# A recommendation tower on one core: gathers on GpSimd spaced by small products, the first pairs' layer 0 moved between slots, and another layout of the pair tiles

## The chip, the cores and the metric

The kernel runs on one core of a Trainium2 chip. The metric is the device time of one execution in microseconds. Five engines matter: TensorE (PE, and PEld for its weight loads), VectorE (DVE), ScalarE (ACT), GpSimd (POOL) and SyncE (SP), which here only issues DMAs.

## The reference, cut to what matters

```python
e = stack([tbl_f[ids[:, f]] for f in range(32)], axis=1)      # [1024, 32, 16], gathered from 32 tables
x0 = xk = e
for W in (W0, W1, W2):                                        # W0 [32, 32, 64], W1 and W2 [32, 64, 64]
    xk = relu(einsum('bmd,bhd,mhk->bkd', x0, xk, W))          # layers 0, 1, 2
    outs.append(sum(xk, axis=2))
h = concatenate([outs..., dense_ctx], axis=1)                 # [1024, 208]
y = relu(relu(h @ W_top1 + b_top1) @ W_top2 + b_top2) @ W_top3
```

Each layer multiplies every field m of x0 with every field h of the state, element by element, and contracts the products with a weight for each (m, h). All of it is float32.

## The kernel before

**Pairs.** The columns (1024 rows of the batch times 16 = 16384) are cut into 16 pairs of 1024 columns, numbered 0 to 15. For each pair p the steps are these.

- *Gathers* (POOL, L325): 16 indirect DMAs, 128 table rows each, into `gath[p % 2]`. In all 256 gathers; those of pair p are numbers 16p to 16p + 15.
- *Store* (SP, L235): when all 16 have landed, `gath` is written twice to scratch in HBM (`x_scratch`, 64 rows of 1024 columns: the 32 fields twice, so that a rotated read needs no wrap). SP then waits for the landing.
- *Loads for layer 0* (SP): `x0c` (L280; for pairs 1 and 2 directly from `gath`, L245), then `x_rep` and two tiles of `x_rot` (L287, L291), 512 KB each. `x_in` counts the landing of these three.
- *Pair tiles* (SP, L298): `m_rep`, four DMAs of 1 MB that lay the 32 fields over 128 partitions, 8 KB for each partition. Three pairs fit in `m_rep`.
- *Layer 0*: a product `x_rot * x_rep` into `prod_pool` (`layer0_product`, for pair 1 on DVE at L417, for all later pairs on POOL at L336); two `pair_sums` on PE (L576, from `x0c`), each squared by ACT (L473); then PE's `layer0_sums` and `layer0_rest` (L596, L640), and ACT's `relu0` (L452).
- *Layers 1 and 2*: for each, ACT (L480) replicates the state into PSUM (`rep`), DVE (L399) multiplies a tile of `m_rep` with `rep`, 128x2048 at a time, and PE (L660) contracts the product in four matmuls. That is a *unit*; 8 units make one layer of one pair. From slot 3 on, one of the 8 is multiplied by POOL (L336, `prod_pool<-m_rep,xb`) from a copy of `rep` in SBUF (`xb`), in slots 29 to 31 two.

**Slots.** One layer of one pair is a slot, and every engine goes through them in the same written order: (layer 1, pair 0), (2, 0), (1, 1), (1, 2), (2, 1), (1, 3), (2, 2), ... So for p from 2 on, slot 2p - 1 is layer 1 of pair p, and slot 2p is layer 2 of pair p - 1. In slot 2p - 1 layer 0 of pair p + 1 is made as well: PE has `pair_sums(p + 1, 0)` after unit 0, `pair_sums(p + 1, 1)` after unit 3, and the rest at the slot's end. Slots 0 to 2 are arranged by hand: layer 0 of pair 1 stands in slot 0 before and behind its last unit (`layer0_sums(1)`, `layer0_rest(1)`), and that of pair 2 at the end of slot 1 and in slot 2.

**Order.** There is no scheduler. Each engine's block is a program of its own, executed in order; semaphores tie them together. POOL's queue holds three things in one order: gathers, its own units, and layer 0 products. A gather that waits, or a product that waits for `x_in`, holds back all that stands behind it. POOL's program in and before the slots is:

```python
gather(0, 16);  wait l0_done >= 1;  gather(16, 16)
for n in range(7):  wait unit_ready >= 2 * n + 1;  gather(32 + 4 * n, 4)
layer0_product(2)
for n in range(7, 10):  wait unit_ready >= 2 * n + 1;  gather(32 + 4 * n, 4)
ahead = 72
for i in range(3, NS):
    odd slot (layer 1, pair p):  units(i); gather(ahead, 4); layer0_product(p + 1); gather(ahead + 4, 2)
    even slot (layer 2):         gather(ahead, 5); units(i); gather(ahead + 5, 5)
```

So 72 gathers are issued before slot 3 is reached, and then 16 for each two slots.

## Time and profile before

| | us |
|---|---|
| median of 3 runs | 660.87 (660.35 to 661.81) |
| the profiled execution's own time | 659.91 |
| its span, first to last instruction | 658.1 |
| PE busy | 602.4 (92%) |
| DVE busy | 528.1 (80%) |
| POOL busy | 453.6 (69%) |
| ACT busy | 391.4 (59%) |

The profile is of one execution. Its times count from the start of its span; 1.81 us of the execution's own time lie outside it. A row of the timeline gives start, duration, engine and line, what is written and read, how many instructions are merged in it, and in brackets the idle time before it with what ended it. "issue" means that nothing the profile shows was waited for, and "remote" that the semaphore's update matches no instruction's recorded end. In the table of stretches each engine has its busy time and count, then follow TensorE's granted clock (1.00 is 2.4 GHz, 0.50 is 1.2 GHz), the share of time for which the DMA engines were busy, and GB/s.

### The profile page before, as it was taken

The numbers are of one execution on the slowest core, as the hardware profiler recorded it, in microseconds if no ns is written. First come the engines' busy times: TensorE is split into PE (matmuls) and PEld (weight loads), VectorE is DVE, ScalarE is ACT, GpSimd is POOL, SyncE is SP. The second block draws the span as 40 slices with busy tenths as digits, with TensorE's granted clock in tenths as the row PEclk, the third lists the DMA queues.
The fourth block names the chain that finished last, engine by engine and source line by source line (L and its number), as shares of the span: only waits on it lengthen the run. The fifth ranks groups of instructions, "written<-read, shape, count | busy, mean of one in ns | idle before, by whom it ended". The sixth has DMA issues, their size and how long they took to land.

```text
span 658.1 us, 7277 instructions
## 1 busy us (share of the span) xinstructions
PE 602.4 (92%) x2634; PEld 192.6 (29%) x2634; DVE 528.1 (80%) x281; ACT 391.4 (59%) x631; POOL 453.6 (69%) x306
## 2 busy tenths in 40 slices
PE   1765497789999999999999999999999999999998
PEld 1211122223333333333333333333333333333343
DVE  1065198499989898999999898989898999899700
ACT  0200254386767676767677776858586867677231
POOL 5367365488989788878788878888598855267300
PEclk9997698989999999999999999999999999999999
DMA  4193969594959595968778695949494939450000
GB/s 134 40 226 71 238 168 248 155 236 112 249 129 238 118 249 127 233 148 211 162 204 177 186 198 162 219 146 218 136 222 113 246 92 248 109 97 0 9 8 1
DMA packets 38413, 103.44 MB, mean 157 GB/s; under 512 B 13764, under 2 KB 22856, under 8 KB 30184
## 3 DMA queue, kind: packets, MB, share of 16 engines
q1 hardware_dynamic: 28900, 98.72, 60.8%
q0 software_dynamic: 8192, 2.11, 3.4%
q10 hardware_dynamic: 1284, 2.13, 1.0%
q8 instruction: 21, 0.34, 0.2%
q14 instruction: 16, 0.13, 0.1%
HBM read 97.69 MB, written 4.20 MB: 155 GB/s over the span
## 4 chain that ended last, share of the span: by engine, by line
PE 84%; another core or an unknown queue 5%; issue 4%; ACT 2%; POOL 2%; ACTq 1%; DVE 1%; DMA 1%; SPq 0%; DVEq 0%; POOLq 0%
PE acc L660 65%; PE pair_sum L596 8%; PE pair_sum L576 5%; POOL gath L325 2%; PE pair_sum L640 2%; PE rep L746 2%; PE rep L738 1%; PE rep L739 1%; ACT rep L480 1%; DVE prod L399 1%; ACTq L445 1%; DMA gath<-in_tables,rows_sb 0%; ACT prod_pool L501 0%; SPq L245 0%
## 5 line engine op out<-in xcount | busy, mean ns | idle before, releaser
L399 DVE TENSOR_TENSOR prod<-m_rep,rep 128x2048 f32<-128x2048 f32 x223 | 494.5, 2281 | 56.3 <-DMA m_rep<-x_scratch 28.5
L660 PE MATMUL acc<-prod,w_sb 128*64 128x512 f32 x1792 | 406.0, 602 | 18.3 <-DVE prod L399 13.7
L480 ACT COPY rep<-state 32x512 f32<-32x512 f32 x488 | 283.4, 581 | 59.3 <-DVE prod L399 43.3
L325 POOL DMA_INDIRECT gath<-in_tables,rows_sb x256 | 243.1, 949 | 101.5 <-issue 75.2
L660 PEld LDWEIGHTS acc<-prod,w_sb 128*64 128x64 f32 x1792 | 124.9, 138 | 290.9 <-issue 274.4
L336 POOL TENSOR_TENSOR prod_pool<-m_rep,xb 128x2048 f32<-128x2048 f32 x32 | 146.3, 4571 | 51.7 <-PE acc L660 26.1
L336 POOL TENSOR_TENSOR prod_pool<-x_rot,x_rep 128x2048 f32<-128x2048 f32 x14 | 64.1, 4578 | 9.4 <-DMA x_rot<-x_scratch 9.2
L660 PE MATMUL acc<-prod_pool,w_sb 128*64 128x512 f32 x256 | 60.4, 592 | 0.0
L473 ACT ACTIVATE sums_sq<-pair_sum 128x1024 f32<-128x1024 f32 x30 | 30.8, 1027 | 45.5 <-PE pair_sum L576 25.4
L452 ACT ACTIVATE state<-pair_sum 128x512 f32<-128x512 f32 x16 | 9.6, 597 | 74.2 <-PE pair_sum L640 58.9
L576 PE MATMUL pair_sum<-x0c,sel_sb 32*128 32x512 f32 x120 | 35.7, 672 | 13.8 <-issue 9.5
L409 DVE TENSOR_REDUCE z_sb<-state 128x32 f32<-128x512 f32 x48 | 32.6, 681 | 19.3 <-ACT state L452 17.5
L596 PE MATMUL pair_sum<-sums_sq,w_sb 128*64 128x512 f32 x128 | 30.3, 594 | 0.0
L490 ACT COPY xb<-rep 128x1024 f32<-128x1024 f32 x29 | 29.4, 1013 | 0.9
L660 PEld LDWEIGHTS acc<-prod_pool,w_sb 128*64 128x64 f32 x256 | 18.4, 137 | 36.5 <-issue 36.5
L596 PE MATMUL pair_sum<-prod_pool,w_sb 128*64 128x512 f32 x120 | 28.3, 592 | 0.0
L452 ACT ACTIVATE state<-acc 128x512 f32<-128x512 f32 x32 | 19.1, 602 | 14.2 <-PE acc L660 14.1
L468 ACT ACTIVATE xsq<-x0c 64x512 f32<-64x512 f32 x15 | 9.5, 631 | 25.0 <-DMA x0c<-gath 24.6
L576 PEld LDWEIGHTS pair_sum<-x0c,sel_sb 32*128 32x128 f32 x120 | 9.4, 191 | 40.2 <-issue 35.0
L640 PE MATMUL pair_sum<-xsq,wdiag_sb 32*64 32x512 f32 x60 | 16.1, 613 | 0.0
L417 DVE TENSOR_TENSOR prod_pool<-x_rot,x_rep 128x2048 f32<-128x2048 f32 x1 | 2.3, 2336 | 15.5 <-issue 15.5
L596 PEld LDWEIGHTS pair_sum<-sums_sq,w_sb 128*64 128x64 f32 x128 | 9.0, 137 | 18.3 <-issue 18.0
(52 smaller groups left out, 102.9 us busy)
## 6 DMA issues: line engine op xcount, KB each, us to landing
m_rep<-x_scratch SPq DMA_DIRECT2D x64, 1024.0 KB
x_rot<-x_scratch SPq DMA_DIRECT2D x30, 512.0 KB
x_rep<-x_scratch SPq DMA_DIRECT2D x15, 512.0 KB
gath<-in_tables,rows_sb POOLq DMA_INDIRECT x256
x_scratch<-gath SPq DMA_DIRECT2D x31, 128.0 KB
x0c<-x_scratch SPq DMA_DIRECT2D x26, 64.0 KB
w_sb<-in_w ACTq DMA_DIRECT2D x2, 512.0 KB
m_rep<-z_sb SPq DMA_DIRECT2D x12, 64.0 KB, 2.3
```

The source lines that it names most:

```text
L325: pool.indirect_dma_start(out=gath[p % 2][:, g, :], out_offset=None, in_=tables, in_offset=bass.IndirectOffsetOnAxis(ap=rows_sb[:, n:n + 1 ...
L336: nc.gpsimd.tensor_tensor(prod_pool[:, at % POOL_RING], in0, in1[:, None, :].to_broadcast([128, 2, PAIR]), ALU.mult).then_inc(pool_ready, 1)
L399: nc.vector.tensor_tensor(prod[:, number % RING], in0, in1[:, None, :].to_broadcast([128, 2, PAIR]), ALU.mult).then_inc(unit_ready, 1)
L409: nc.vector.tensor_reduce(out=z_sb[l][:, p, :], in_=state[l][:, :].rearrange("k (b d) -> k b d", d=D), op=ALU.add, axis=AX_X).then_inc(z_r ...
L452: nc.scalar.activation(state[l][:, :], acc_of[l][:, :], RELU).then_inc(state_ready[l], 1)
L473: nc.scalar.activation(sums_sq[:, n, :], pair_sum[:, :], SQUARE).then_inc(sq_ready, 1)
L480: last = nc.scalar.copy(rep[v][M * q:M * q + M, CHUNK * a:CHUNK * a + CHUNK], state[l - 1][K * a + M * v:K * a + M * v + M, :])
L490: nc.scalar.copy(xb[i % 2][:, :], rep[0][:, :]).then_inc(xb_ready, 1)
L576: last = nc.tensor.matmul(pair_sum[:, CHUNK * a:CHUNK * a + CHUNK], sel_sb[M * a:M * a + M, n, :], x0c[p % 2][M * a:M * a + M, :], start=T ...
L596: last = nc.tensor.matmul(acc0[K * a:K * a + K, :], w, src[:, CHUNK * a:CHUNK * a + CHUNK], start=start, stop=stop)
L640: last = nc.tensor.matmul(acc0[K * a:K * a + K, :], wdiag_sb[M * a:M * a + M, :], xsq[M * a:M * a + M, :], start=False, stop=True)
L660: last = nc.tensor.matmul(acc[K * a:K * a + K, :], w, src[:, k, CHUNK * a:CHUNK * a + CHUNK], start=start and k == 0, stop=stop and k == 1)
```

## The change

Six edits:

1. POOL's gathers ahead of slot 3. Gathers 16 to 19 are issued as soon as the first squares are there (`first_sq`), before `l0_done`. The other gathers up to number 63 no longer wait for `unit_ready`: they go in blocks of four (`BURST`), and behind each block of four POOL makes a product of 128x256 elements of weights into a tile `unread` that nobody reads; each such product waits for the one before it. `ahead` starts at 4 * 16 = 64 where it was 72.
2. The layer 0 product of pair 2 goes from POOL to DVE, in slot 2 behind its unit 3. That of pair 1, which is DVE's already, goes from the start of slot 1 to behind slot 1's unit 1.
3. PE's layer 0 of pair 1 goes out of slot 0 into slot 1 (`pair_sums` behind `copy_state(1, 0)` and unit 0, sums behind unit 2, rest behind unit 3); that of pair 2 lies wholly within slot 2.
4. ACT's order follows: `relu_slot(0)` ahead of the squares of pair 1, `replicate(1, 1)` between them.
5. In slot 3 alone PE makes the `pair_sums` of pair 3 behind units 2 and 4, not 0 and 3.
6. `m_rep`: partition n holds the fields n // 4 + t, not 2 * (n // 8) + t. The DMA reads 32 starts with 4 copies of each, 4 KB apart, 8 KB each (they overlap), where it read 16 starts with 8 copies. The bytes are the same, and the weights are laid out to match.

```diff
-                    src = bass.AP(row.tensor, row.offset, [[2 * PAIR, 128 // T], [0, T], [1, 2 * PAIR]])
+                    src = bass.AP(row.tensor, row.offset, [[PAIR, M], [0, Q], [1, 2 * PAIR]])
...
             gather(0, FIRST_RUN)
+            pool.wait_ge(first_sq, 1)
+            gather(FIRST_RUN, BURST)
 
             pool.wait_ge(l0_done, 1)
-            gather(FIRST_RUN, 2 * GPP - FIRST_RUN)
-
-            for n in range(7):
-                pool.wait_ge(unit_ready, 2 * n + 1)
-                gather(2 * GPP + 4 * n, 4)
-            layer0_product(2)
-            for n in range(7, 10):
-                pool.wait_ge(unit_ready, 2 * n + 1)
-                gather(2 * GPP + 4 * n, 4)
-            ahead = 72
+            pool.wait_ge(w1_in, 16)
+            ahead = 4 * GPP
+            for k, n in enumerate(range(FIRST_RUN + BURST, ahead, BURST)):
+                gather(n, BURST)
+
+                after(pool, burst_out, k)
+                nc.gpsimd.tensor_tensor(unread[:, :, :], w_sb[1][:, 0, 0:T // 2, :], w_sb[1][:, 1, 0:T // 2, :],
+                                        ALU.mult).then_inc(burst_out, 1)
...
+                    if (i, n) in ((1, 1), (2, 3)):
+                        layer0_product(i)
...
             relu0(0)
+            relu_slot(0)
             square_x(1)
             square(1, 0)
+            replicate(1, 1)
             square(1, 1)
-            relu_slot(0)
-            replicate(1, 1)
```

On POOL, from slot 3 to the start of slot 7 (`gath0` takes the gathers of even pairs, `gath1` those of odd ones). Before:

```order
L325 DMA gath0<-in_tables,rows_sb 128x16 x3
L336 TENSOR_TENSOR prod_pool<-m_rep,xb1 128x2048 [waits l0_done,m_in2_3,xb_ready]
L325 DMA gath0<-in_tables,rows_sb 128x16 x4
L336 TENSOR_TENSOR prod_pool<-x_rot,x_rep 128x2048 [waits pool_used,x_in]
L325 DMA gath0<-in_tables,rows_sb 128x16 x4
L325 DMA gath1<-in_tables,rows_sb 128x16 [waits x0_stored]
L325 DMA gath1<-in_tables,rows_sb 128x16 x2
L336 TENSOR_TENSOR prod_pool<-m_rep,xb0 128x2048 [waits pool_used,m_in1_3,xb_ready]
L325 DMA gath1<-in_tables,rows_sb 128x16 x5
L336 TENSOR_TENSOR prod_pool<-m_rep,xb1 128x2048 [waits pool_used,m_in0_3,xb_ready]
L325 DMA gath1<-in_tables,rows_sb 128x16 x4
L336 TENSOR_TENSOR prod_pool<-x_rot,x_rep 128x2048 [waits pool_used,x_in]
```

And the same stretch now:

```order
L340 TENSOR_TENSOR prod_pool<-m_rep,xb1 128x2048 [waits l0_done,m_in2_3,xb_ready]
L329 DMA gath0<-in_tables,rows_sb 128x16 [waits x0c_in0,x0_stored]
L329 DMA gath0<-in_tables,rows_sb 128x16 x3
L340 TENSOR_TENSOR prod_pool<-x_rot,x_rep 128x2048 [waits l0_done,x_in]
L329 DMA gath0<-in_tables,rows_sb 128x16 x7
L340 TENSOR_TENSOR prod_pool<-m_rep,xb0 128x2048 [waits pool_used,m_in1_3,xb_ready]
L329 DMA gath0<-in_tables,rows_sb 128x16 x5
L340 TENSOR_TENSOR prod_pool<-m_rep,xb1 128x2048 [waits pool_used,m_in0_3,xb_ready]
L329 DMA gath1<-in_tables,rows_sb 128x16 [waits x0_stored]
L329 DMA gath1<-in_tables,rows_sb 128x16 x3
L340 TENSOR_TENSOR prod_pool<-x_rot,x_rep 128x2048 [waits pool_used,x_in]
```

The first product with `x_rot` is that of pair 3, the last row's is that of pair 4. Before, the last gather of pair 4 was the fourth behind pair 3's product, and between it and pair 4's own product stood 12 gathers of pair 5 and two units. Now the last gather of pair 4 stands directly ahead of slot 5's unit, and that unit and four gathers are all that lies between it and pair 4's product. The same holds for every later pair.

On PE, from the units 5 and 6 of slot 0 into slot 1. Before:

```order
39 L576 MATMUL pair_sum<-x0c,sel_sb 128x512 [waits state_ready0,x0c_in1]
40 L576 MATMUL pair_sum<-x0c,sel_sb 128x512
41 L660 MATMUL acc<-prod,w_sb 64x512 [waits unit_ready]
42 L660 MATMUL acc<-prod,w_sb 64x512 x3
43 L576 MATMUL pair_sum<-x0c,sel_sb 128x512 [waits sq_ready,x0c_in1]
44 L576 MATMUL pair_sum<-x0c,sel_sb 128x512
45 L660 MATMUL acc<-prod,w_sb 64x512 [waits tile_ready]
```

And now:

```order
39 L667 MATMUL acc<-prod,w_sb 64x512 [waits unit_ready]
40 L667 MATMUL acc<-prod,w_sb 64x512 x3
41 L667 MATMUL acc<-prod,w_sb 64x512 [waits tile_ready]
42 L667 MATMUL acc<-prod,w_sb 64x512
43 L667 MATMUL acc<-prod,w_sb 64x512 [waits unit_ready]
44 L667 MATMUL acc<-prod,w_sb 64x512
45 L658 MATMUL rep<-state,xb 128x512 [waits unit_ready,state_ready1]
46 L658 MATMUL rep<-state,xb 128x512
47 L583 MATMUL pair_sum<-x0c,sel_sb 128x512 [waits state_ready0,x0c_in1]
```

The last units of slot 0 no longer stand behind a wait for pair 1's data; that wait now stands in slot 1.

## Rows read from the trace of the kernel before

**Rows 1.** Stretches: busy us and count by engine, clock, DMA share, GB/s:

```profile
200.00:300.00 100.00, 100.00 (x454) 31.45 (x452) 94.78 (x51) 72.80 (x118) 83.64 (x56) 1.00 0.75 179
```

**Rows 2.** Who waited for whom, 0 to 120 us: total, times, longest:

```profile
ACT sums_sq L473 <- remote: 18.1, 2, 13.4
```

**Rows 3.** The chain that ended last, slots 25 to 27: start, us, what:

```profile
516.99 1.06 PE pair_sum L576 x4
518.05 5.30 PE acc L660 x24
...
551.46 1.06 PE pair_sum L576 x4
```

**Rows 4.** The timeline, POOL in slots 4 to 6:

```profile
149.85 0.94 POOL L325 DMA_INDIRECT gath<-in_tables,rows_sb  x1 [0.30 <-issue]
...
165.27 4.57 POOL L336 TENSOR_TENSOR prod_pool<-m_rep,xb 128x2048 f32<-128x2048 f32 x1
...
174.74 4.60 POOL L336 TENSOR_TENSOR prod_pool<-x_rot,x_rep 128x2048 f32<-128x2048 f32 x1
...
197.74 0.94 POOL L325 DMA_INDIRECT gath<-in_tables,rows_sb  x1 [0.30 <-issue]
```

**Rows 5.** The timeline: pair 1's last gather; SP's queue, pairs 1, 4:

```profile
53.21 0.94 POOL L325 DMA_INDIRECT gath<-in_tables,rows_sb  x1 [0.30 <-issue]
...
55.55 0.60 SPq L245 DMA_DIRECT2D x0c<-gath  x1
...
155.25 1.16 SPq L235 DMA_DIRECT2D x_scratch<-gath  x2
160.03 0.78 SPq L280 DMA_DIRECT2D x0c<-x_scratch  x2
160.85 0.57 SPq L287 DMA_DIRECT2D x_rep<-x_scratch  x1
```

**Rows 6.** The timeline: loads for layer 0 of pair 15, what waited for them:

```profile
542.63 0.58 SPq L287 DMA_DIRECT2D x_rep<-x_scratch  x1
...
550.99 4.56 POOL L336 TENSOR_TENSOR prod_pool<-x_rot,x_rep 128x2048 f32<-128x2048 f32 x1 [3.98 <-DMA x_rot<-x_scratch]
...
551.39 1.13 PE L576 MATMUL pair_sum<-x0c,sel_sb 32*128 32x512 f32 x4
```

**Rows 7.** The timeline: start-up, from pair 0's layer 0 to slot 3:

```profile
34.49 0.94 POOL L325 DMA_INDIRECT gath<-in_tables,rows_sb  x1 [10.39 <-PE pair_sum L596]
...
55.29 2.35 DVE L405 TENSOR_TENSOR prod<-m_rep,rep 128x1024 f32<-128x1024 f32 x2
...
73.18 2.34 DVE L417 TENSOR_TENSOR prod_pool<-x_rot,x_rep 128x2048 f32<-128x2048 f32 x1 [15.54 <-issue]
...
81.98 15.47 DVE L399 TENSOR_TENSOR prod<-m_rep,rep 128x2048 f32<-128x2048 f32 x7 [6.46 <-PE rep L651]
...
86.56 0.60 ACT L452 ACTIVATE state<-pair_sum 128x512 f32<-128x512 f32 x1 [1.06 <-PE pair_sum L640]
...
90.89 4.73 ACT L480 COPY rep<-state 32x512 f32<-32x512 f32 x8 [3.73 <-issue]
...
94.88 0.59 SPq L287 DMA_DIRECT2D x_rep<-x_scratch  x1
...
104.43 4.54 POOL L336 TENSOR_TENSOR prod_pool<-x_rot,x_rep 128x2048 f32<-128x2048 f32 x1 [5.22 <-DMA x_rot<-x_scratch]
...
130.82 1.01 ACT L490 COPY xb<-rep 128x1024 f32<-128x1024 f32 x1
...
131.91 4.54 POOL L336 TENSOR_TENSOR prod_pool<-m_rep,xb 128x2048 f32<-128x2048 f32 x1 [8.07 <-ACT xb L490]
```

**Rows 8.** Stretches: pair tiles alone; loads for layer 0; clock behind a pause:

```profile
137.00:152.00 15.00, 15.00 (x68) 4.49 (x66) 15.00 (x8) 12.20 (x19) 12.70 (x10) 0.99 0.99 218
545.00:550.00 5.00, 5.00 (x26) 1.58 (x22) 5.00 (x4) 4.74 (x9) 2.02 (x1) 1.00 0.95 325
103.00:107.00 4.00, 3.76 (x10) 1.07 (x12) 4.00 (x3) 3.71 (x7) 2.57 (x1) 0.57 1.02 231
```

More of the change, by code:

```diff
@@ L32 @@
 FIRST_RUN = 16
+BURST = 4
 WARM_FROM = 10
@@ L65, in sums_to, with sums_at @@
     return QB * (p - 1)
-SUMS_AT = (0, 3)
+def sums_at(i):
+    return (2, 4) if i == POOL_FROM else (0, 3)
 def order(i):
@@ L76, in order @@
     return [(0, u) for u in range(v0_units(i))] + [(1, u) for u in range(4)]
-POOL_SEQ = [("x", 2)]
+POOL_SEQ = []
 for _i in range(POOL_FROM, NS):
@@ L188, in build @@
         diag_half = sem("diag_half")
-        second_x = sem("second_x")
+        early_x = sem("early_x")
         xsq_ready = sem("xsq_ready")
@@ L202, in build @@
         z_in = [sem(f"z_in{i}") for i in range(2)]
+        burst_out = sem("burst_out")
         top_ready = sem("top_ready")
@@ L219, in x_multiplied @@
         def x_multiplied(eng, p):
-            if p == 1:
-                eng.wait_ge(second_x, 1)
+            if p <= 2:
+                eng.wait_ge(early_x, p)
             else:
@@ L332, in product @@
                 if at < POOL_RING:
-                    pool.wait_ge(l0_done, at + 1)
+                    pool.wait_ge(l0_done, at + 2)
                 else:
@@ L410, in sum_d, with layer0_product @@
                                         op=ALU.add, axis=AX_X).then_inc(z_ready[l], 1)
+            def layer0_product(p):
+                dve.wait_ge(x_in, 16 * (1 + XT) * (p - EARLY + 1))
+                nc.vector.tensor_tensor(prod_pool[:, p - 1], x_rot[:, :, :], x_rep[:, None, :].to_broadcast([128, XT, PAIR]),
+                                        ALU.mult).then_inc(early_x, 1)
             for i, (l, p) in enumerate(SLOTS):
                 base, nv = UNIT_BASE[i], v0_units(i)
-                if i == 1:
-                    dve.wait_ge(x_in, 16 * (1 + XT))
-                    nc.vector.tensor_tensor(prod_pool[:, 1], x_rot[:, :, :], x_rep[:, None, :].to_broadcast([128, XT, PAIR]),
-                                            ALU.mult).then_inc(second_x, 1)
                 if i >= POOL_FROM:
@@ L632, in layer0_rest @@
                 x_multiplied(pe, p)
-                at = 1 if p == 1 else POOL_AT[("x", p)] % POOL_RING
+                at = p - 1 if p <= 2 else POOL_AT[("x", p)] % POOL_RING
                 for t in range(XT):
                     last = layer0_tile(w0_sb[:, t, :], prod_pool[:, at, t, :], False, False)
-                if p > 1:
+                if p > 2:
                     last.then_inc(pool_used, 1)
@@ L706, in _ @@
                         pool_unit(0)
-                    if i >= 3 and l == 1 and p + 1 < NP and n in SUMS_AT:
-                        pair_sums(p + 1, SUMS_AT.index(n))
-                    if i == 0 and n in (5, 6):
-                        pair_sums(1, n - 5)
+                    if i >= 3 and l == 1 and p + 1 < NP and n in sums_at(i):
+                        pair_sums(p + 1, sums_at(i).index(n))
                     if (i, n) == (0, 7):
                         copy_state(1, 0)
-                        layer0_sums(1)
-                        layer0_rest(1)
-                    if (i, n) == (1, 7):
-                        pair_sums(2, 0)
-                    if (i, n) == (2, 1):
-                        pair_sums(2, 1)
-                    if (i, n) == (2, 2):
-                        layer0_sums(2)
-                    if (i, n) == (2, 3):
-                        layer0_rest(2)
+                        pair_sums(1, 0)
+                    if (i, n) == (1, 0):
+                        pair_sums(1, 1)
+                    if i == 2 and n in (1, 2):
+                        pair_sums(2, n - 1)
+                    if (i, n) in ((1, 2), (2, 3)):
+                        layer0_sums(i)
+                    if (i, n) in ((1, 3), (2, 4)):
+                        layer0_rest(i)
                 if pooled:
```

3 lines of the change are left out of this document (2 added, 1 removed).

## The prediction

> **What bounds the kernel now.** I read the table of stretches first. In a stretch amid the run PE is busy for all of 100 us at a granted clock of 1.00, DVE for 95 [rows 1]. The chain of work that ended last agrees: from slot 25's `pair_sums` to slot 27's it is PE without a gap, 34.47 us for the two slots of one pair (551.46 - 516.99), and a unit takes PE 1.77 us (5.30 / 3) [rows 3]. From about 140 us to the end PE is the bound.
>
> Next to it stands an engine that is nearly as full. POOL shows 84% [rows 1], but the 0.30 us between two gathers is its own issue time, not a wait. The timeline of POOL gives a round: from pair 4's product at 174.74 to the end of the last of the next 12 gathers and one unit at 198.68 it is 23.94 us, and from a unit of an odd slot over four gathers to the product 9.47 us (165.27 to 174.74) [rows 4]. Together that is 33.4 of PE's 34.47 us. POOL has 1 us to spare for each pair.
>
> Before 140 us nothing is full. The waits there name what: ACT sat 13.4 us for PE's first `pair_sums` of pair 1 [rows 2], because PE and ACT have this pair's layer 0 written into slot 0, ahead of slot 0's last unit. DVE was through with slot 0 at 57.64 and started slot 1 at 81.98 [rows 7].
>
> **The change at the start-up: a gain.** The prices are from [rows 7] unless another group stands beside them: a unit on DVE 2.21 us (15.47 / 7), `relu` 0.60, replicate 4.73, `xb` 1.01.
>
> Slot 0. DVE's last row still ends at 57.64. PE no longer stands behind pair 1: half a unit (0.9), `relu` (0.6) and a copy of the state by PE (four matmuls of 128x512, an estimate of 0.9 from half a unit) let slot 1 start at about 60.2 instead of 81.98.
>
> Gathers. Twelve of pair 1's gathers follow the 34.49 mark instead of 16, and two small products lie between them. A small product has an eighth of the elements of a 128x2048 product of 4.57 us [rows 4], so 0.57 us, and with a 0.15 us change of instruction 0.7 us; as the wait in it is for the product before, long done, it hides nothing else, and 1.5 us is the upper end. The last gather ends at 34.49 + 12 x 1.25 - 0.3 + 1.4 = 50.6 instead of 54.15 [rows 5], so all that hangs on it comes 3.5 us earlier: pair 1's product at 73.18 - 3.5 = 69.7.
>
> Slot 1. DVE makes two units until 64.6 and waits for `x_in`; the product ends at 72.0; two more units at 76.5. PE takes the sums of layer 0 (1.77), unit 3 (1.77) and the rest (1.77 + 0.9, priced as units) until 82.2; `relu` and replicate let slot 2 start at 87.5. DVE's remaining units end at 85.3 and are covered.
>
> Slot 2. Four units (8.8) and two sums over the state (a quarter of a unit each by elements, 1.1) reach 97.4. If `x_in` of pair 2 has landed by then, the product (2.34), one unit (2.21), PE's unit and rest (4.4), `relu`, replicate and `xb` (6.3) start slot 3 at 112.8 instead of 131.9. The product was POOL's and cost DVE nothing before; here it lies on the path. POOL's product of pair 3 then could start at 112.8 + 9.47 = 122.3.
>
> **The layout of `m_rep`.** This decides how soon the loads of pairs 2 and 3 come, since they queue behind 4.19 MB of pair tiles. While pair tiles alone move, the rate is 218 GB/s; while `x_rep` and `x_rot` move it is 325 [rows 8]. `x_rep` is read from 32 starts with four copies of each, which is what `m_rep` now gets; it was 16 starts with eight. One bound is 325 GB/s (12.9 us for a pair), the other is that the 8 KB pieces are the cause and nothing changes (19.2 us). I take the first, as the pattern is the same as that of the fast rows. Then `x_in` of pair 2, 104.43 before [rows 7], is at 104.4 - 3.5 - 6.3 = 94.6, in time, and pair 3's at 94.6 + 12.9 + 4.78 + 0.82 + 8.36 = 121.5 (the last three as below), in time too. With the slow rate they are at 100.9 and 134, and pair 3's product waits until 134. The steady part does not care: PE was full while DMA was at 75% [rows 1]. The other edits I cost at nothing: the four gathers ahead of `l0_done` run on an otherwise idle POOL (10.39 us [rows 7]), ACT's new order only moves squares behind a `relu` that is due first, and slot 3's `pair_sums` stand later, where their `x0c` is nearer to landed; if that cover is gone, PE waits at most the us by which `x0c` is late there.
>
> **What the change takes away: eight gathers of lead.** `ahead` is 64, not 72. POOL's program from slot 3 on is the same text, so every gather stands 8 places later against the products. The last gather of pair 4 was issued at 149.85 [rows 4]; now it takes the place directly ahead of slot 5's unit, at 164.3. From there to pair 4's product POOL has 9.47 us of work. What must happen meanwhile:
> - the gather lands: 54.15 to 55.55 [rows 5], 1.40 us;
> - SP stores twice and waits: 155.25 to 160.03, 4.78 us; `x0c` is issued: 0.82 us [rows 5];
> - `x_rep` and `x_rot` are issued and land: 542.63 to 550.99, 8.36 us, at a place where POOL waited for just that [rows 6].
>
> That is 15.36 us against 9.47: POOL stands still for 5.9 us in each odd slot, and all behind it in its queue is the next pair's last 12 gathers. So it does not catch up. The loop closes over itself: product, 12 gathers and a unit (23.94), then 15.36, then the next product: **39.3 us for a pair, against PE's 34.47**. Before, only four gathers lay between a product and the next pair's last gather, so the same loop took 4.6 + 0.15 + 4 x 1.25 + 15.4 = 25 us, below PE's round. Idle time on an engine that is not the bottleneck costs nothing, but here POOL becomes the bottleneck. PE feels it first at `pair_sums` behind unit 0 of the odd slots, which needs `x0c`; its four matmuls hold back the units queued behind.
>
> **The sum.** From pair 3's product to pair 15's are 12 rounds: 471.6 us. Pair 15's `x0c` lands, by the parts of the 8.36 us that are not data (3.5 us of 8.36, the rest being 1.57 MB at 325 GB/s), 2 to 4 us after its issue, so about 6 us ahead of the product; from that `pair_sums` at 551.39 to the span's end were 106.7 us [rows 6], all PE. So the end lies 100.7 us behind pair 15's product. PE's pause of 5 us will also pull its clock down, as behind the shorter pause near 103 us, where the clock was 0.57 over 4 us [rows 8]: 1.7 us lost, once, since in the other rounds POOL's loop hides it. Span: 122.3 + 471.6 + 100.7 + 1.7 = 696.3. With 1.8 us outside the span 698.1, and as the median lies 1.0 us over the profiled execution, **699.1 us**. With the slow rate of pair tiles (134): 710.8.
>
> Each leg has another row: 9.55 us for the loads (94.88 to 104.43 [rows 7]), which would make the loop 40.5 and add 14 us; and nothing below 8.36 that a wait shows, though 0.3 us less would follow from a slightly higher rate, 4 us in all.
>
> **Rivals.**
> - *The leg is covered.* If the way from gather to product took at most 9.5 us, POOL would never wait, PE would stay full, and only the start-up counts: 660.9 - (131.9 - 112.8) = 642. It decides at 9.5 us; the rows say 15.4, and each of its four parts was taken where its own queue was free. Chance 0.05.
> - *The leg shrinks but is not covered.* Of the stores' 4.78 us some 4.0 are not data (0.26 MB at 325 GB/s are 0.8), of the loads' 8.36 some 3.5. With nothing else in the queue these parts might fall, say by half, which makes the leg 11.6 and the loop 35.5 us; the break-even is a loop of (660.9 - 2.8 - 102.4 - 122.3) / 12 = 36.1 us, a leg of 12.2, and at 35.5 the time is 653. For it: PE and the other traffic were busy in the rows. Against: the 8.36 us row had no other large transfer beside it either. Chance 0.03.
> - *The start-up gain does not come*, because the runs of gathers or a landing hold PE and ACT as at 60 to 73 us [rows 2] in the new order too: product of pair 3 at 141 as before, time 718. Chance 0.12.
> - *Slow pair tiles*, 711: 0.27. *The forecast*, 699 with its bounds: 0.51. The rest, 0.02, is no difference.
>
> The Trainium skill, "DMA: Bandwidth & Descriptors", section "Anatomy of one DMA", gives a transfer about 2.0 us plus its bytes at 436 GB/s, fitted on GpSimd's DMAs. An estimate by that page is 2.6 us for the stores and 5.6 us for the loads, which is the second rival's leg of 11.6 and its 653 us; the rows have 4.78 and 8.36 with the issue, and the trace decides against it.
>
> **Numbers.** The range takes in the forecast with the loop's bounds and the slow tiles, and most of the third rival: 690 to 718. What can be told from no change is 0.2%, 1.3 us. Faster 0.08, same 0.02, slower 0.90.
>
> **What would show it.** Right: slot 3's `xb` at 113 to 116; products with `x_rot` on POOL 39 us apart from pair 4 on, each behind a wait of about 6 us for `x_rot`; PE pauses of 3 to 5 us before L583 in odd slots only, behind `x0c`; PE's busy share near 86%; pair tiles moving at over 300 GB/s. Wrong: products 34.5 us apart (the first rival), a wait in POOL other than for `x_rot`, PE pausing elsewhere, or slot 3 at 130.

## The result: 6% slower, and the profile after

The changed kernel takes 700.49 us (median, 697.11 to 701.57), the kernel before, run beside it, 660.61 us. The ratio is 1.0598, 95% interval 1.0554 to 1.0642. The profiled execution took 700.23 us, its span is 698.4 us. The forecast was 699.1.

The page of the changed kernel: busy times, PE and its clock over the span in 40 slices, the DMA queue of SP, and the chain of work that ended last.

```profile
PE 626.1 (90%) x2634; PEld 198.1 (28%) x2634; DVE 531.2 (76%) x282; ACT 392.2 (56%) x631; POOL 460.1 (66%) x316
...
PE   1776877999979899998999898998999799999998
...
PEclk9999888899989899998999999898999899999999
...
q1 hardware_dynamic: 28900, 98.72, 37.7%
...
POOL 37%; DMA 24%; issue 17%; PE 15%; SPq 5%; ACT 1%; ACTq 0%; DVE 0%; POOLq 0%
...
```

PE falls from nearly every slice full to eights and nines with dips, and POOL now leads the chain with 37%, followed by DMA with 24%. In the middle of the run, where PE was 100% busy at clock 1.00 [rows 1], a stretch of the same length reads:

```profile
200.00:300.00 100.00, 93.86 (x392) 28.93 (x392) 81.31 (x42) 63.20 (x101) 70.70 (x48) 0.92 0.52 186
```

Who waits for whom between 160 and 600 us (total, times, longest). In the kernel before, POOL waited for `x_rot` once in this stretch, 4.0 us, and ACT and PE never for `x0c`:

```profile
POOL prod_pool L340 <- DMA x_rot<-x_scratch: 72.6, 12, 10.4
...
ACT xsq L475 <- DMA x0c<-x_scratch: 44.3, 11, 5.9
...
DVE z_sb L413 <- ACT state L459: 31.2, 9, 3.7
PE pair_sum L583 <- DMA x0c<-x_scratch: 26.5, 10, 4.6
```

Twelve waits of POOL for `x_rot`, one for each pair, 6.05 us on average. (The last, 10.4 us, is pair 15's, which has no gathers left in front of its product; the other eleven average 5.7 us.) One round on POOL's timeline, with SP's queue beside it, answers [rows 4] and [rows 5, 6] (start, us, and in brackets the idle time before):

```profile
287.06 4.57 POOL L340 TENSOR_TENSOR prod_pool<-x_rot,x_rep 128x2048 f32<-128x2048 f32 x1 [6.14 <-DMA x_rot<-x_scratch]
...
300.27 4.57 POOL L340 TENSOR_TENSOR prod_pool<-m_rep,xb 128x2048 f32<-128x2048 f32 x1
305.00 0.98 POOL L329 DMA_INDIRECT gath<-in_tables,rows_sb  x1 [0.16 <-issue]
...
310.04 0.95 POOL L329 DMA_INDIRECT gath<-in_tables,rows_sb  x1 [0.31 <-issue]
311.01 4.59 POOL L340 TENSOR_TENSOR prod_pool<-m_rep,xb 128x2048 f32<-128x2048 f32 x1
...
319.54 0.94 POOL L329 DMA_INDIRECT gath<-in_tables,rows_sb  x1 [0.30 <-issue]
326.20 4.56 POOL L340 TENSOR_TENSOR prod_pool<-x_rot,x_rep 128x2048 f32<-128x2048 f32 x1 [5.71 <-DMA x_rot<-x_scratch]
```

SP's queue in this round (the same columns):

```profile
312.50 1.16 SPq L239 DMA_DIRECT2D x_scratch<-gath  x2
317.26 0.77 SPq L284 DMA_DIRECT2D x0c<-x_scratch  x2
318.08 0.57 SPq L291 DMA_DIRECT2D x_rep<-x_scratch  x1
```

The last gather of the pair starts at 310.04, directly ahead of the odd slot's unit, and its row ends at 310.99. The stores follow at 312.50, `x0c` at 317.26, `x_rep` at 318.08, and the product starts at 326.20, 15.2 us behind the end of the gather's row. POOL had 9.5 us of work for that (to 320.48). The products with `x_rot` stand at 287.06 and 326.20, 39.1 us apart, where PE needs 34.47 [rows 3].

The start-up, which was to give some of this back, is shorter but not by as much as forecast. On the timeline, PE's first `pair_sums` of pair 2, and two rows of ACT around their squares:

```profile
94.89 1.13 PE L583 MATMUL pair_sum<-x0c,sel_sb 32*128 32x512 f32 x4
...
93.23 0.63 ACT L475 ACTIVATE xsq<-x0c 64x512 f32<-64x512 f32 x1
99.68 1.02 ACT L480 ACTIVATE sums_sq<-pair_sum 128x1024 f32<-128x1024 f32 x1 [5.82 <-remote]
```

and the first row of POOL in slot 3:

```profile
119.89 4.55 POOL L340 TENSOR_TENSOR prod_pool<-m_rep,xb 128x2048 f32<-128x2048 f32 x1 [21.23 <-ACT xb L497]
```

POOL's product of pair 3 starts at 129.34; it was at 141.34 before and forecast for 122.3.

### The profile page after: what moved, and what is told of

It reads as the page before. It is cut to its first block, busy times and chain, and to the rows that moved or that the text cites. A ratio compares the mean times of both kernels' runs of the same rounds, so it can differ in the third digit from the quotient of the medians.

```text
span 698.4 us, 7287 instructions
## 1 busy us (share of the span) xinstructions
PE 626.1 (90%) x2634; PEld 198.1 (28%) x2634; DVE 531.2 (76%) x282; ACT 392.2 (56%) x631; POOL 460.1 (66%) x316
## 3 DMA queue, kind: packets, MB, share of 16 engines
q1 hardware_dynamic: 28900, 98.72, 37.7%
## 4 chain that ended last, share of the span: by engine, by line
POOL 37%; DMA 24%; issue 17%; PE 15%; SPq 5%; ACT 1%; ACTq 0%; DVE 0%; POOLq 0%
POOL gath L329 24%; POOL prod_pool L340 12%; DMA x_rot<-x_scratch 11%; PE acc L667 9%; DMA x_scratch<-gath 7%; DMA gath<-in_tables,rows_sb 5%; PE rep L750 2%; SPq L284 1%; SPq L239 1%; SPq L295 1%; PE pair_sum L603 1%; PE rep L742 1%; PE rep L743 1%; SPq L291 1%; POOL unread L367 1%
## 5 line engine op out<-in xcount | busy, mean ns | idle before, releaser
L667 PE MATMUL acc<-prod,w_sb 128*64 128x512 f32 x1792 | 423.1, 623 | 18.8 <-DVE prod L403 13.7
L329 POOL DMA_INDIRECT gath<-in_tables,rows_sb x256 | 246.1, 961 | 79.7 <-issue 66.9
L667 PEld LDWEIGHTS acc<-prod,w_sb 128*64 128x64 f32 x1792 | 129.0, 143 | 308.8 <-issue 286.4
L340 POOL TENSOR_TENSOR prod_pool<-x_rot,x_rep 128x2048 f32<-128x2048 f32 x13 | 59.3, 4563 | 72.6 <-DMA x_rot<-x_scratch 72.6
L583 PE MATMUL pair_sum<-x0c,sel_sb 32*128 32x512 f32 x120 | 40.4, 755 | 30.7 <-DMA x0c<-x_scratch 26.5
L413 DVE TENSOR_REDUCE z_sb<-state 128x32 f32<-128x512 f32 x48 | 32.6, 681 | 44.2 <-ACT state L459 39.3
L682 PE MATMUL acc<-w_sb 128*64 128x512 f32 x10 | 6.6, 826 | 8.6 <-DMA gath<-in_tables,rows_sb 8.6
```

The source lines that it names most:

```text
L329: pool.indirect_dma_start(out=gath[p % 2][:, g, :], out_offset=None, in_=tables, in_offset=bass.IndirectOffsetOnAxis(ap=rows_sb[:, n:n + 1 ...
L340: nc.gpsimd.tensor_tensor(prod_pool[:, at % POOL_RING], in0, in1[:, None, :].to_broadcast([128, 2, PAIR]), ALU.mult).then_inc(pool_ready, 1)
L413: nc.vector.tensor_reduce(out=z_sb[l][:, p, :], in_=state[l][:, :].rearrange("k (b d) -> k b d", d=D), op=ALU.add, axis=AX_X).then_inc(z_r ...
L583: last = nc.tensor.matmul(pair_sum[:, CHUNK * a:CHUNK * a + CHUNK], sel_sb[M * a:M * a + M, n, :], x0c[p % 2][M * a:M * a + M, :], start=T ...
L667: last = nc.tensor.matmul(acc[K * a:K * a + K, :], w, src[:, k, CHUNK * a:CHUNK * a + CHUNK], start=start and k == 0, stop=stop and k == 1)
```

## Experiments

The runs fell on three chips, called B, C and D here (the result above is from another, A). Each chip was used in one session, so what is said of a chip below could also be of its session. The kernel before has a trace from A alone. The kernel before ran beside them on each: 664.35 us on B, 654.57 on C, 661.22 on D. Ratios are to the kernel before on the same chip, and are what is to be compared; "product 3" is the start of POOL's product with `x_rot` of pair 3, a mark for the end of the start-up. The first group is about the loop, the second about the start-up. All kernels compute everything.

**The lead put back to 72 gathers** (chip B).

```
-            ahead = 4 * GPP
+            ahead = 72
...
-                gather(n, BURST)
+                gather(n, min(BURST, ahead - n))
```

> The changed kernel with ahead = 72: two more blocks of four gathers (64 to 71), each with its small product, stand ahead of slot 3, and nothing else differs. Lead theory: the last gather of a pair again stands two units and 12 gathers ahead of the pair's product, POOL never waits for x_rot, products on POOL stand 34.5 us apart, PE is full from slot 3 on. Slot 3 starts at 119.9 us in the changed kernel against 131.9 before, so the time is 660.6 - 12 = 649. Rival (small products, the pair 2 product on DVE or the new tile layout cost the time, not the lead): it stays at 690 to 700, with POOL's waits for x_rot gone but PE still pausing.

Measured: 659.27 us, 0.9921 (0.9884 to 0.9958). POOL does not wait for `x_rot` any more; PE is full from 140 us, and products are 34.0 us apart on average (140.69 to 549.25, 12 rounds). So the lead alone made the loss. But the time is 10 us above what was expected: product 3 is at 140.69, as late as before. See the second group.

**A lead of 66** (chip B), the same edit with 66.

> The changed kernel with ahead = 66: two gathers of lead given back of the eight. Lead theory, in numbers: two gathers are 2.5 us more work between a pair's last gather and its product, so the loop is 39.07 - 2.5 = 36.6 us, twelve rounds 439 us, and the time 129.3 + 439 + 100.3 + 1.8 = 670, POOL waiting 3.5 us for x_rot in each odd slot. A rival in which POOL's wait is a matter of queueing in the DMA rings and not of the order on POOL gives no proportional step: 700, or 649 at once.

Measured: 677.73 us, 1.0213 (1.0143 to 1.0284), 8 us above what was expected, of which 4.9 are a later product 3 (134.15, not 129.3). The waits shrink and the rounds come down to 36.8 us (134.15 to 575.89 in 12 rounds, by the products):

```profile
POOL prod_pool L340 <- DMA x_rot<-x_scratch: 46.5, 12, 9.9
```

Two more gathers between a product and the next pair's last gather take 2.5 us off POOL's work in the loop by the closed loop of the forecast; measured are 2.2 (rounds 39.06 - 36.81; waits 6.05 - 3.88). The loss is a matter of degree, as the closed loop says, not a switch.

**The kernel before with a lead of 64** (chip B): one part of the change alone.

```
-            for n in range(7, 10):
+            for n in range(7, 8):
                 pool.wait_ge(unit_ready, 2 * n + 1)
                 gather(2 * GPP + 4 * n, 4)
-            ahead = 72
+            ahead = 64
```

> The kernel before with only the lead taken away: gathers 64 to 71 are not issued ahead of slot 3 and ahead = 64. Lead theory: product of pair 3 at 141.3 as before, then twelve rounds of 39.1 and 100.3 us to the end: 141.3 + 469 + 100.3 + 1.8 = 712. Rival (the other edits cost it): 661, no change.

Measured: 737.59 us, 1.1117 (1.105 to 1.1185), 26 us more than expected. The sign is right: the lead alone, in the old kernel, costs more than the whole change. The size is off, since the rounds here are 41.0 us long (144.49 to 636.82, 12 rounds), not 39.1, and POOL waits 7.7 us for `x_rot` (84.5 us in 11). Two kernels with the same lead differ by 2 us per pair, so something else in the change helps the loop.

**The changed kernel with the old layout of `m_rep`** (chip C) names it.

```
-                    src = bass.AP(row.tensor, row.offset, [[PAIR, M], [0, Q], [1, 2 * PAIR]])
+                    src = bass.AP(row.tensor, row.offset, [[2 * PAIR, 128 // T], [0, T], [1, 2 * PAIR]])
...
-        return np.asarray(w).reshape(M, 2 * M, K)[(n // Q + t) % M, M * v + n % M]
+        return np.asarray(w).reshape(M, 2 * M, K)[(2 * (n // T) + t) % M, M * v + n % M]
```

> The changed kernel with its lead of 64 gathers, and with the former layout of m_rep alone put back; everything is computed as before. The kernel before with a lead of 64 took 41.1 us per pair where the changed kernel takes 39.1. Theory A (it is the layout: with the slower tiles the loads of x0c, x_rep and x_rot lie behind tiles still under way, and the waits for x_rot are 7.7 instead of 6.05 us in an odd slot): pairs 41 us apart here too, 12 x 2.0 = 24 us more than 700.5, so 718 to 730. Theory B (it is the spacing or the order in the start-up, and the loop does not feel the layout): 39.1 per pair and 698 to 706.

Measured: 726.45 us, 1.1091 (1.1049 to 1.1132), as theory A has it. Rounds of 40.9 us (135.46 to 626.53), and POOL's waits between 160 and 600 us:

```profile
POOL prod_pool L340 <- DMA x_rot<-x_scratch: 84.0, 11, 9.4
```

A long round on the timeline, SP's queue:

```profile
409.36 0.78 SPq L284 DMA_DIRECT2D x0c<-x_scratch  x2
410.18 0.58 SPq L291 DMA_DIRECT2D x_rep<-x_scratch  x1
```

and POOL's product behind it:

```profile
421.42 4.57 POOL L340 TENSOR_TENSOR prod_pool<-x_rot,x_rep 128x2048 f32<-128x2048 f32 x1 [8.85 <-DMA x_rot<-x_scratch]
```

From `x0c` to the product it is 12.06 us here and between 9.06 and 12.06 in the five rounds from 285 to 463 us; in the changed kernel it is 8.31 to 9.55 in the same stretch. The bytes of `x_rep` and `x_rot` and their pattern are the same in both. What differs is what SP issues behind them: one of a pair's four tile transfers of 1 MB takes 18.8 us from issue to landing here and 10.0 in the changed kernel (medians of those from 270 to 420 us whose landing the trace has; in the changed kernel these are three). Those of one pair, issued from 333.74 on, have all landed here at 358.81, before the next pair's `x0c` is issued at 370.07, so nothing of them lies ahead of these loads. The tiles stand on the chain that ended last in this kernel, by engine and by line:

```profile
DMA 44%; PE 23%; POOL 16%; SPq 7%; issue 6%; DVE 2%; ACT 1%; ACTq 0%; POOLq 0%; DVEq 0%
DMA m_rep<-x_scratch 26%; PE acc L667 16%; POOL gath L329 12%; DMA x_scratch<-gath 9%; DMA gath<-in_tables,rows_sb 6%; POOL prod_pool L340 4%; SPq L302 3%; PE pair_sum L603 2%; DVE prod L403 2%; PE rep L750 2%; SPq L295 1%; PE pair_sum L583 1%; DMA x_rot<-x_scratch 1%; PE rep L742 1%; PE rep L743 1%
```

In the changed kernel's chain the tiles are not among the leading items. So the layout is worth 4.7% (1.1091 against 1.0598, on two chips) with a lead of 64. The timelines tell by which way. Averaged over the 12 rounds, the way from `x0c` to the product is 8.85 us in the changed kernel and 10.78 here, while the rest of the leg is the same (gather to stores 1.4, stores to `x0c` 4.9 and 4.8); the 1.9 us are the whole difference of the rounds. The pair of kernels on chip B says the same without a change of chip: 8.94 us with the new layout (lead 66) and 10.88 with the old (the kernel before, lead 64). So the layout works in the loop by how soon `x_rot` lands. In the start-up it works too: up to slot 3 this kernel and the one with eight gathers behind the squares (chip C as well, below) differ in the layout alone, save for those eight gathers, and slot 3 starts at

```profile
123.55 4.54 POOL L340 TENSOR_TENSOR prod_pool<-m_rep,xb 128x2048 f32<-128x2048 f32 x1 [24.90 <-ACT xb L497]
```

here and at 114.89 there, and product 3 at 135.46 and 124.34.

**The lead of 72 with the old layout** (chip C), both edits together.

> The changed kernel with a lead of 72 gathers and with the former layout of m_rep; everything is computed as before. With 72 gathers of lead the way of a pair to its x_rot (store, x0c, x_rep, x_rot) is covered, so POOL should not wait for x_rot in the loop and PE should be full from about 140 us, with 34.5 us per pair, by either theory. They differ in the start-up. Theory A (the new layout makes the tiles' loads faster, 12.9 against 19.2 us a pair, and the start-up is the shorter for it): the tiles of pair 1 and 2 land some 6 us later, the time is 662 to 668 against 659.3 for the same kernel with the new layout. Theory B (fast tiles crowd the gathers' own work in the queues, as the kernel before with the new layout alone came out slower, 671.2 against 664.4): the old layout is the better one here too, 650 to 656. Theory C (with gathers spaced out by products the layout plays no part in the start-up): 658 to 661.

Measured: 647.61 us, 0.9897 (0.9872 to 0.9922). With the lead in place the loop does not feel the layout; the eight rounds from 135.63 to 403.10 are 33.4 us long, which is POOL's full round of 33.4 us by [rows 4]. On ratios the run is at the edge of theory C, and the old layout lies between the kernels with the new one on chips B and D (0.9921 above and 0.9805 below). But on its own chip the kernel with the new layout and the eight gathers behind the squares takes 643.56 us, 4.1 us less, and starts slot 3 at 114.89 instead of 122.17; POOL stood idle for 11.6 us before that, so the place of the gathers isn't what held slot 3 here. Where the lead is there, the layout counts in the start-up only, by some 4 us in this comparison, in which the place of the eight gathers differs too.

The second group is about the start-up. In the first kernel above (lead 72, chip B) ACT's first squares of pair 2 waited for PE until POOL's gathers were over, though PE's record of these `pair_sums` ends at 96.38. ACT on the timeline:

```profile
111.77 1.02 ACT L480 ACTIVATE sums_sq<-pair_sum 128x1024 f32<-128x1024 f32 x1 [17.86 <-remote]
```

and the last of the gathers on POOL:

```profile
109.23 0.94 POOL L329 DMA_INDIRECT gath<-in_tables,rows_sb  x1 [0.30 <-issue]
110.19 0.73 POOL L367 TENSOR_TENSOR unread<-w_sb 128x256 f32<-128x256 f32 x1
```

**The kernel before with the new layout alone** (chip B, and again on D); the edit is that above, reversed, in the kernel before.

> The kernel before with only the new layout of m_rep (32 starts with 4 copies, weights laid out to match). My theory: pair tiles alone move at over 300 GB/s instead of 218 to 238, slot 0 ends about 3 us earlier, but pair 1's x0c holds PE there as before; pair 2's and 3's loads come some 6 us earlier, of which 2 to 5 us reach slot 3: 656 to 659. Rival (the layout costs or gives nothing at the start): 660.6 within 1.3.

Measured: 671.17 us, 1.0171 (1.01 to 1.0242): the wrong side. PE and ACT stand still between 65 and 80 us. ACT's first squares of pair 1, which started at 73.53 in the kernel before (a wait of 13.4 us [rows 2]), on the timeline:

```profile
80.19 1.02 ACT L473 ACTIVATE sums_sq<-pair_sum 128x1024 f32<-128x1024 f32 x1 [20.24 <-remote]
```

and the stretch 60 to 80 us:

```profile
60.00:80.00 20.00, 4.74 (x12) 0.77 (x8) 2.29 (x1) 0.00 (x0) 12.05 (x12) 0.59 0.81 285
```

PE's matmuls for these sums are recorded as ended at 61.42, so the signal came 18.8 us behind them (11.9 before). In both kernels POOL issues 32 gathers back to back, from 34.5 to 74 or 75 us. With the faster tiles DMA moves 285 GB/s in this stretch beside the gathers' own small packets, where it was 204, and the last of the gathers' packets ends at 79.4, just ahead of the release. (In the kernel before it ends at 81.4, 7.9 us behind the release at 73.53, so the packets alone don't set it.)

> The kernel before with the new layout of m_rep alone, a second time; on the first chip it took 671.2 us against 664.4, ratio 1.0171, with PE's signal of the pair sums of pair 1 arriving 18.8 us behind their end (11.9 in the kernel before). Theory A (fast tiles only lengthen that hold, and the hold is what is different between chips): on a chip where signals come in time the tiles of pairs 0 to 2 land sooner, PE waits less for them, and the ratio is 0.985 to 1.0; where they come late, 1.01 to 1.02 again. Theory B (the new layout costs time by itself, by crowding out the gathers): 1.01 to 1.02 on any chip.

Measured on D: 665.02 us, 1.0028 (1.0004 to 1.0052). The signal was again 18.0 us late (61.64 to 79.66). So this edit alone brings nothing on chips B and D, where signals are late; neither of the two expectations is met exactly, and how far the layout by itself would help where signals come in time was not run.

**Without the small products**, lead 72 (chip C, and again on D): is the spacing of any use?

```
                 gather(n, min(BURST, ahead - n))
-
-                after(pool, burst_out, k)
-                nc.gpsimd.tensor_tensor(unread[:, :, :], w_sb[1][:, 0, 0:T // 2, :], w_sb[1][:, 1, 0:T // 2, :],
-                                        ALU.mult).then_inc(burst_out, 1)
```

> The changed kernel with a lead of 72 gathers and without the small products between the blocks of four; everything is computed as before. The traces show that PE's signal to ACT after the pair sums of pair 1 comes 12 us after PE's recorded end in the kernel before (at 73.5 us, where its run of gathers ends at 74.1), 19 us after it where the tiles of pair 1 load at 285 GB/s, and 1.6 us after it in the changed kernel, where products stand between the gathers. Theory A (signals of PE are held while gathers are issued back to back, until the run ends): here one run of 52 gathers of 1.25 us follows from 35 to about 100 us, so the squares of pair 1 wait until near 100 us, slot 1 starts some 30 to 45 us later than at 58, and the time is 685 to 705. Theory B (the products only cost 0.74 us each and hold nothing together): 13 of them go, POOL is through 9.6 us earlier, and the time is 650 to 659.

Measured on C: 640.98 us, 0.9795 (0.977 to 0.982). This spoke for theory B: 52 gathers in one run, and no signal of PE late.

> The changed kernel with a lead of 72 and without the small products, a second time; the first gave 641.0 us, 0.9795 of the kernel before on its chip. Theory A (the products are for chips on which PE's signals are held while gathers run back to back): on such a chip this kernel's slot 1 starts 20 us or more later than at 60 us and the ratio is above 1.0 (52 gathers of 1.25 us in one run); on a chip where signals come in time, 0.978 to 0.982 again. Theory B (the products do nothing for the signals on any chip): 0.978 to 0.985 on either.

Measured on D, the same program: 687.2 us, 1.0378 (1.0338 to 1.0419). The stretches from 60 to 100 us (busy us of PE, PE's weight loads, DVE, ACT, POOL, then clock, DMA share, GB/s) on C:

```profile
60.00:80.00 20.00, 14.27 (x52) 4.06 (x52) 16.37 (x9) 5.61 (x10) 15.43 (x16) 0.83 0.84 303
80.00:100.00 20.00, 18.54 (x82) 5.46 (x82) 14.76 (x9) 12.56 (x20) 15.59 (x15) 1.00 0.85 302
```

with ACT's `relu` ahead of slot 1 on the timeline:

```profile
56.11 0.60 ACT L456 ACTIVATE state<-acc 128x512 f32<-128x512 f32 x1 [21.13 <-PE acc L664]
```

This is theory A, on the chip for which it was said. On D the stretches:

```profile
60.00:80.00 20.00, 3.18 (x8) 0.42 (x4) 0.58 (x1) 0.00 (x0) 15.13 (x17) 0.50 0.85 307
80.00:100.00 20.00, 0.00 (x0) 0.00 (x0) 0.00 (x0) 0.00 (x0) 14.96 (x16) 0.50 0.08 12
```

and PE's last row of slot 0, with the same `relu` behind it:

```profile
59.50 3.68 PE L664 MATMUL acc<-prod,w_sb 128*64 128x512 f32 x8 [4.86 <-issue]
...
108.20 0.60 ACT L456 ACTIVATE state<-acc 128x512 f32<-128x512 f32 x1 [72.93 <-remote]
```

On D PE, DVE and ACT stand still from 63 to 108 us. The `relu` for which all wait needs PE's last matmuls of slot 0, whose recorded end is 63.18: the signal is 45 us late. It comes 8.7 us behind the end of the run of gathers (99.52); on C the `relu` goes at 56.11. The two runs are of one program, so the program doesn't decide which of the two happens; the chip does, or what else differed between the sessions. On chips A, B and D every profile has a signal of PE to ACT that comes 3 to 45 us behind the recorded end, while in C's four profiles none of ACT's waits for PE between 40 and 140 us ends more than 0.1 us behind it.

**Eight gathers moved behind the squares of pair 2** (chip C): the lead of 72, but the last 8 gathers in the gap in which POOL waited for `xb`.

```
+            pool.wait_ge(sq_ready, 4)
+            gather(ahead, 8)
+            ahead += 8
             for i in range(POOL_FROM, NS):
```

> The changed kernel as it is up to the 64th gather, and then 8 more (to a lead of 72) in one run that begins only when the squares of pair 2 are done (103.9 us in the changed kernel's trace), in the 21.2 us in which POOL waited for xb of slot 3; everything is computed as before. Theory A (the lead alone makes the loop's loss, and the late slot 3 of the kernel with 72 gathers in front, 131.2 us against 119.9, came of PE's signals being held by the two further blocks, since ACT's square waited 17.9 us until the gathers ended): slot 3 starts at 120 to 122, no waits for x_rot follow, pairs 34.5 us apart, the product of pair 3 on POOL at 130, the span 659.3 less 9 to 11: 648 to 651. Theory B (slot 3 is late for another reason, by the loads or by PE's clock, whatever the place of the 8 gathers): 656 to 660, the same as with 72 in front. A third outcome would be that the run holds PE's last signal before slot 3 (recorded at 113.3 us), by up to 2 us: 650 to 653.

Measured: 643.56 us, 0.9832 (0.9806 to 0.9857). Slot 3 starts at 114.9, product 3 at 124.34, and the rounds are 34.1 us on average (124.34 to 533.91, 12 rounds). POOL on the timeline:

```profile
101.39 0.98 POOL L329 DMA_INDIRECT gath<-in_tables,rows_sb  x1 [2.68 <-ACT sums_sq L483]
...
114.89 4.55 POOL L340 TENSOR_TENSOR prod_pool<-m_rep,xb 128x2048 f32<-128x2048 f32 x1 [3.76 <-ACT xb L500]
...
124.34 4.56 POOL L340 TENSOR_TENSOR prod_pool<-x_rot,x_rep 128x2048 f32<-128x2048 f32 x1
```

The expected times go with chip B's 664 us; by the ratio they are 0.975 to 0.980 for theory A, up to 0.983 for the third outcome, 0.987 to 0.993 for B. By the number it came out at the third, but not by its cause, as PE's last signal before slot 3 isn't late here. And since signals come in time on C in all four kernels, this run does not tell why the kernel with 72 in front started slot 3 late on B.

**The lead of 72 in front, again** (chip D), and **both edits** (8 behind the squares, no products; chip D).

> The changed kernel with a lead of 72 gathers, all in front of slot 3, in blocks of four with products between, a second time, beside the next three kernels. In the runs so far PE's signals came late (up to 15 us behind the recorded end of the matmul, until the gathers' run was over) in all kernels of one chip, the one on which this kernel was 0.9921 of the kernel before, and in none of the kernels of the other chip, on which 8 gathers behind the squares gave 0.9832. Theory A (the 8 gathers in front cost nothing by themselves where the signals come in time): slot 3 starts at most 2 us later than with them behind the squares, and the ratio is within 0.005 of that of the next run with products. Theory B (the place of the 8 gathers matters on every chip): 0.990 to 0.994, slot 3 10 us later. Where signals are late on this chip too, A and B give the same.

Measured: 650.26 us, 0.9805 (0.9747 to 0.9863); slot 3 at 124.2, product 3 at 133.61. ACT's squares of pair 2 waited 9.39 us for PE, and went at 103.74, amid the gathers, behind one of them that took 2.12 us instead of 0.94; on B the same program had waited 17.86 us, until they were over. So with 8 more gathers in front the same program starts slot 3 at 131.3 on B and 124.2 on D; what makes the signal come before or behind the end of the gathers is not known. As signals are late on D too, the run doesn't part the two theories: the ratio is as good as that with the gathers behind the squares on C, at a start of slot 3 that is 9 us later, and the interval is wide.

> The changed kernel without the small products, with the gathers up to 64 back to back, and 8 more once the squares of pair 2 are done; everything is computed as before. With products the same took 0.9832 of the kernel before, and without products but with 72 in front 0.9795. Theory A (where signals come in time the products cost 0.74 us each and the gathers' end sets pair 1 and 2, so that both edits do the same thing): 0.978 to 0.981, no faster than 0.9795. Theory B (both gains add up): 0.972 to 0.977. Where signals come late on this chip: above 1.0 if unspaced gathers hold them, as the run of 32 in the kernel before does.

Measured: 678.4 us, 1.0237 (1.0192 to 1.0282), above 1.0, as was expected where signals are late. Without products the first run ends 8 gathers earlier than in the kernel without them and with 72 in front, at 89 us instead of 99.5, and the `relu` ahead of slot 1 goes 11.8 us earlier (96.36 against 108.20). ACT on the timeline:

```profile
96.36 0.60 ACT L459 ACTIVATE state<-acc 128x512 f32<-128x512 f32 x1 [61.70 <-remote]
```

POOL's next gather waited for the squares since the end of the run at 88.9:

```profile
136.17 0.94 POOL L329 DMA_INDIRECT gath<-in_tables,rows_sb  x1 [47.27 <-ACT sums_sq L480]
```

The `relu`'s signal is 40 us late here (PE's last matmul of slot 0 ends at 56.16). The run of gathers ends 10.6 us earlier and the hold 11.8 us earlier, so the hold moves with the run.

## Why the prediction held, point by point

**The closed loop: right.** The forecast had a leg of 15.36 us from the end of the last gather's row to the product against 9.47 us of cover; the rows above have 15.2 (stores 4.76, `x0c` 0.82, loads 8.12, landing and start of the stores 1.5). It had 5.9 us of waiting in each odd slot; there are 12 waits of 6.05 us on average, 5.7 without the last. It had 39.3 us a round; there are 39.06 ((598.10 - 129.34) / 12). The lead of 66 gave a step in between and the lead of 72 none, which shows the cause, and the lead of 64 in the kernel before shows that it needs nothing else of the change.

**The start-up: the mechanism right, the size off by 7 us.** Slot 1 started at 57.84 (forecast 60.2, as DVE's two waits for tiles, 2.9 us, were gone as well), pair 1's product at 68.39 (69.7), slot 2 at 88.48 (87.5), but slot 3 at 119.9 (112.8), and with it product 3 at 129.34 (122.3). The step that failed is slot 2: "the product (2.34), one unit (2.21), PE's unit and rest (4.4)" assumed that ACT's squares of pair 2 are due by then. They started at 99.68, 3.7 us behind the recorded end of the `pair_sums` (96.02), with PE at a granted clock of 0.50 from 101 to 104 us, behind that pause. On chip C, where no signal is late, slot 3 starts at 114.9. So some 5 of the 7 us are the late signal and what follows from it, and 2 are the sum's own; that split compares two chips and two kernels and is no more than an estimate. (Two of the sum's own steps don't add up as written: slot 1's start comes to 60.0, not 60.2, and PE's part of slot 1 to 82.7, not 82.2. Neither matters for the result.)

**The layout: the right end chosen, for the wrong part.** Tiles did move fast (98.72 MB took 37.7% of the DMA engines, 60.8% before), faster than the 325 GB/s taken: 426 GB/s in a stretch with little else. Slow tiles were priced at 711 us by the start-up alone, as "the steady part does not care". With the loop closed over `x_rot` it does care: the run with old tiles has rounds of 40.9 us and a ratio of 1.1091, which is 733 us on the chip of the result (660.61 x 1.1091), 32 us above the changed kernel, not 12. The forecast's 11.7 us for the start-up were right: product 3 is 11.1 us later with old tiles on chip C (135.46 against 124.34). The term that was put at nothing is the 1.9 us in each round, 22 us in twelve.

**The small terms.** The end behind pair 15's product is 100.3 us (forecast 100.7 and 1.7 for the clock, which was not lost there); the small products took 0.74 us each (0.7). The sum: 696.3 + 7.0 (start-up) - 2.8 (rounds) - 2.1 (end) = 698.4. The closeness of the total to its forecast is in part luck, since 7 us late and 5 us early cancel.

**The rivals.** *The leg is covered* is out: 15.2 us. *The leg shrinks*: the stores still took 4.76 us and the loads 8.12, with little else in the queue. By the fit in the Trainium skill, "DMA: Bandwidth & Descriptors", "Anatomy of one DMA", which is for single DMAs issued by GpSimd, an estimate is 2.6 and 5.6 us; the trace of the changed kernel disagrees for these chains on SP's queue, as that of before did. The forecast equated this estimate with its rival's leg of 11.6 us, which is a slip: with 2.6 and 5.6 in place of 4.78 and 8.36 the leg is 10.4 and the loop 34.4, just under PE's 34.47. *The start-up gain does not come* was the rival with the truest mechanism: it named PE and ACT held by the runs of gathers, and on chips B and D that is what one sees, yet in the changed kernel on chip A it cost some 5 us and not 19.

**What of the change is good.** The account by product 3 and pair 15's product is -12.0 us (141.34 to 129.34) for the start-up, +59.1 for the 12 rounds (468.8 against 550.99 - 141.34 = 409.65), and -6.8 for the end (100.3 against 107.1): +40.3, the difference of the spans (698.4 - 658.1). With the lead back, the kernel is a little faster than the kernel before: 0.9921 and 0.9805 of it on B and D with all 72 in front, 0.9832 on C with 8 of them behind the squares.

## What to carry to other kernels

When a change takes gathers or loads off a prefetch distance, follow one item around the loop, from its last issue to the first use of what hangs on it, and compare that leg with the work that the waiting engine has in between; an engine at 84% with 1 us to spare becomes the bound as soon as the leg is longer than its cover by more than that, and it stays so since what it waits for is behind its own queue. Price a faster transfer in the loop that it sits in, not only at the start: here the tiles behind the critical loads set how fast these landed. And judge an edit of start-up timing on more than one chip (one program took 0.9795 and 1.0378 here), each time against the kernel before on the same chip.

## What the runs showed of the hardware

- **Signals of PE were late by up to 45 us while GpSimd issued indirect gathers back to back, on three of four chips.** One and the same program: 0.9795 with the `relu` at 56.11 us on C, 1.0378 with it at 108.20 on D. Chip and session weren't separated. On D, products of 0.74 us between blocks of four gathers put the `relu` back to 56.20, for 13 x 0.74 = 9.6 us of POOL's time; on all four chips kernels with these products had it at 56.0 to 60.0 and PE's signal of pair 1's first sums at most 2.1 us late. But they don't end the hold altogether: in the same kernels on A, B and D the signal of pair 2's first sums is still 3.3 to 15.4 us late. What holds the signals isn't settled. In the run with lead 72 on D the release comes 6.5 us ahead of the end of POOL's gathers. In the other kernels the longest hold ends between 0.6 us ahead of that end (kernel before) and 8.7 us behind it (no products, D), and between 7.9 us ahead of the last gather packet and 7.6 us behind it (the same two).
- **The same bytes read with 32 starts and four copies of each load faster than with 16 starts and eight**: a tile transfer of 1 MB took 18.8 us from issue to landing in the old layout and 10.0 in the new one (medians), and stretches in which little but tiles moves had 229 and 426 GB/s. A stretch of the changed kernel with the old layout, and one of the changed kernel:

```profile
342.00:350.00 8.00, 8.00 (x38) 2.50 (x36) 7.93 (x4) 6.22 (x11) 6.63 (x6) 1.00 1.02 229
```

```profile
325.00:333.00 8.00, 8.00 (x36) 2.36 (x34) 7.32 (x4) 6.25 (x10) 6.36 (x3) 0.93 1.01 426
```

DMA engines are full in both (share 1.02 and 1.01).
- **Loads took longer with slow transfers issued behind them**: `x0c` to landed `x_rot` took 8.3 to 9.6 us with fast tiles behind, 9.1 to 12.1 with slow ones (285 to 463 us), with no tiles of the pair before still under way in the rounds looked at.
